# One transformer layer with attention and routed experts: how VectorE inverts the softmax sums and assigns expert slots

## The reference

```
q = x Wq                     16 heads of 64;  latent = x Wkv_down (64 columns)
k, v = latent Wk_up, latent Wv_up
attn = softmax(mask(q k^T / 8));  y = attn v;  x = layernorm(x + y Wout)
probs = softmax(x w_router)  32 experts;  top1 = argmax;  gate = probs[top1]
pos = rank of the token among those of its expert (cumsum of the one-hot rows) - 1
slot = top1 * 320 + pos      where pos < 320, else dropped
out = (silu(buf w_gate[e]) * (buf w_up[e])) w_down[e] for the 320 rows of each expert e
x = layernorm(x + out[slot] * gate, or x alone where dropped)
```

## Time and profile before

| | |
|---|---|
| Time, median of 3 runs | 2606.3 us (2603.69 to 2608.29) |
| The profiled execution's own time | 2605.42 us |
| Its span | 2603.4 us |
| Busy: TensorE, VectorE, GpSimd, ScalarE | 2364.8, 1697.2, 1678.0, 1029.3 us |
| TensorE's mean granted clock | 0.96 of full speed |
| VectorE's copies L1150 in all | 210.6 us in 256 |

### The profile page before, as it was taken

The page is one execution under the profiler, slowest core; times in us unless marked ns, Lnnn a source line. Parts: engine busy times, 40 slices in busy tenths (PEclk is TensorE's granted clock), DMA queues, the critical chain, the costliest instruction groups (busy, mean ns, idle before and its releaser), DMA issues.

```text
span 2603.4 us, 36668 instructions
## 1 busy us (share of the span) xinstructions
PE 2364.8 (91%) x11528; PEld 1519.9 (58%) x11528; DVE 1697.2 (65%) x4490; ACT 1029.3 (40%) x1992; POOL 1678.0 (64%) x1623
## 2 busy tenths in 40 slices
PE   6899998999988998999889998899899988959996
PEld 5555575556655665557555664566555755546774
DVE  4677667676676667776767677666777576434554
ACT  3444424443344434442444344443444244312222
POOL 1677656766677767765777667766687577722444
PEclk8999999999999999999999999999899999969998
DMA  3122100200011001100020001100110001215662
GB/s 84 58 62 70 46 13 13 66 17 17 13 41 42 17 13 25 58 17 13 13 66 18 17 14 43 39 17 13 25 58 17 13 13 49 74 39 163 187 194 67
DMA packets 96816, 118.95 MB, mean 46 GB/s; under 512 B 12288, under 2 KB 75782, under 8 KB 96624
## 3 DMA queue, kind: packets, MB, share of 16 engines
q1 hardware_dynamic: 89712, 99.98, 14.0%
q0 software_dynamic: 6912, 16.64, 1.8%
HBM read 46.91 MB, written 37.90 MB: 33 GB/s over the span
## 4 chain that ended last, share of the span: by engine, by line
PE 54%; POOL 21%; issue 14%; DVE 5%; ACT 1%; POOLq 0%; DMA 0%; DVEq 0%; SPq 0%; ACTq 0%
PE value_ps L721 13%; POOL half_sums L503 12%; PE turned_ps L698 6%; PE misc_ps L743 6%; PE turned_ps L890 5%; PE turned_ps L701 5%; PE misc_ps L620 4%; PE row_ps L673 4%; POOL probs L478 3%; PE misc_ps L733 3%; PE turned_ps L673 2%; POOL slots_x L535 2%; POOL half_sums L498 2%; POOL headsT L510 1%; DVE rinv_rows L1154 1%
## 5 line engine op out<-in xcount | busy, mean ns | idle before, releaser
L963 ACT ACTIVATE probs<-turned_ps 128x512 f32<-128x512 f32 (+2 forms) x1280 | 652.5, 554 | 806.0 <-PE turned_ps L701 787.6
L503 POOL TENSOR_TENSOR half_sums<-half_sums,probs 128x1024 f32<-128x1024 f32 (+3 forms) x512 | 829.6, 1620 | 33.2 <-ACT probs L963 15.9
L721 PE MATMUL value_ps<-probs,lat_keys 128*64 128x512 f32 (+3 forms) x3072 | 610.7, 513 | 70.9 <-POOL probs L478 66.3
L698 PE MATMUL turned_ps<-q_hl,lat_hi 128*128 128x512 f32 (+2 forms) x1280 | 534.5, 418 | 1.5 <-ACT fold_v L1008 1.5
L478 POOL TENSOR_SCALAR_AFFINE_SELECT probs<-probs 128x256 f32<-128x256 f32 x512 | 208.3, 407 | 465.1 <-ACT probs L963 464.3
L701 PE MATMUL turned_ps<-q_max,lat_lo 65*128 65x512 f32 (+2 forms) x1280 | 486.5, 380 | 2.8 <-DMA q_max<-both_rows 2.8
L1116 DVE CUSTOM_DVE_ANT_0 masked_row<-row_ps,future 128x512 bf16<-128x512 f32 (+4 forms) x707 | 346.9, 511 | 150.4 <-PE row_ps L673 144.4
L721 PEld LDWEIGHTS value_ps<-probs,lat_keys 128*64 128x64 f32 x3072 | 185.0, 139 | 357.5 <-issue 203.7
L673 PE MATMUL row_ps<-lat_hi,q_hl 128*128 128x512 f32 (+4 forms) x1026 | 321.0, 353 | 48.7 <-DVE unit_max L1116 37.0
L498 POOL TENSOR_TENSOR half_sums<-probs 128x768 f32<-128x768 f32 (+1 forms) x128 | 269.2, 2103 | 136.2 <-ACT probs L963 113.3
L698 PEld LDWEIGHTS turned_ps<-q_hl,lat_hi 128*128 128x128 f32 x1280 | 248.1, 194 | 166.7 <-issue 100.6
(11 more groups left out here) (192 smaller groups left out, 2664.7 us busy)
## 6 DMA issues: line engine op xcount, KB each, us to landing
q_max<-q_hl SPq DMA_DIRECT2D x256, 128.0 KB
slots_x<-router SPq DMA_DIRECT2D x8, 1290.0 KB, 5.9
ex_x<-slots_x SPq DMA_DIRECT2D x64, 129.0 KB, 2.3
x_in<-in_L_attn_x_bld SPq DMA_DIRECT2D x8, 1024.0 KB, 5.5
layer_out<-x_in SPq DMA_DIRECT2D x8, 1024.0 KB, 4.6
ex_w<-in_L_ffn_w_gate SPq DMA_DIRECT2D x32, 256.0 KB, 3.8
ex_w<-in_L_ffn_w_up SPq DMA_DIRECT2D x32, 256.0 KB, 3.7
ex_w<-in_L_ffn_w_down SPq DMA_DIRECT2D x32, 256.0 KB, 4.5
```

What stands on the lines that cost most here:

```text
L503: nc.gpsimd.tensor_tensor(total, total, now[:, :, q0:BANK], ALU.add).then_inc(added, 1)
L698: nc.tensor.matmul(scores_of(n, h), lat_hi[b % 2][:, keys], q_hl[gp % 2][:, heads, cols], start=True, stop=False)
L721: mm = nc.tensor.matmul(value_ps[h * LD:(h + 1) * LD, q0:BANK], lat_keys[b % 2][:, j, :], probs[:, n % NPROBS, h, q0:BANK], start=(j == 0) ...
L963: nc.scalar.activation(probs[:, n % NPROBS, heads, q0:BANK], scores_of(n, h), ACT.Exp).then_inc(exp_done, 1)
```

## The change

In `invert_rows` the one reciprocal of 128 partitions, the wait behind it and the two copies become four reciprocals of 32 partitions each, straight from `sums_cols`: for each head the group of the half c is read twice and written once onto itself and once onto the head's other group. The transposes wait for all four.

`place` is cut into three functions. `place` (pair 3, t = 7) keeps the product that frees the bank, now first, and two sums over experts. `count_tiles` (pair 3, t = 9, after `low_q`) has the counts, their addition to `earlier` and the inverse of the router's sum. `destinations` (pair 3, t = 11) has the rest. For the last batch all three stand one behind the other.

```diff
                 wait_emptied(dve, ("sums", gp))
-                nc.vector.reciprocal(rinv[:, c, :], sums_cols[:, :].rearrange("p (n q) -> p n q", q=32)[:, :, 0]
-                                     ).then_inc(inverse_done, 1)
-                dve.wait_ge(inverse_done, 3 * n + 1)
+                cols = sums_cols[:, :].rearrange("p (n q) -> p n q", q=32)[:, :, 0]
                 for h in range(2):
-                    src, dst = (64 * h + 32 * k for k in (c, 1 - c))
-                    nc.vector.tensor_copy(rinv[dst:dst + 32, c, :], rinv[src:src + 32, c, :]).then_inc(inverse_done, 1)
-                dve.wait_ge(inverse_done, 3 * n + 3)
+                    src = slice(64 * h + 32 * c, 64 * h + 32 * c + 32)
+                    for k in range(2):
+                        dst = slice(64 * h + 32 * k, 64 * h + 32 * k + 32)
+                        nc.vector.reciprocal(rinv[dst, c, :], cols[src]).then_inc(inverse_done, 1)
+                dve.wait_ge(inverse_done, 4 * (n + 1))
...
                 dve.wait_ge(gate_exp, b + 1)
-                step(nc.vector.tensor_reduce(rt[:, 1, :], work_b[:, :, :], AX.X, ALU.add))
-                settle()
-                step(nc.vector.reciprocal(rt[:, 2, :], rt[:, 1, :]))
                 bank = wait_full(dve, use)
                 nc.vector.tensor_tensor(work_a[:, :, :], onehot[:, :, :],
                                         bank[:, 0:NT * E].rearrange("p (t e) -> p t e", e=E), ALU.mult
                                         ).then_inc(free_of(use), 1)
+                step(nc.vector.tensor_reduce(rt[:, 1, :], work_b[:, :, :], AX.X, ALU.add))
                 wait_emptied(dve, use)
+                step(nc.vector.tensor_reduce(rt[:, 4, :], work_a[:, :, :], AX.X, ALU.add))
+
+            def count_tiles(b):
 
                 step(nc.vector.tensor_reduce(in_tiles[:, :], onehot[:, :, :].rearrange("p t e -> p e t"), AX.X, ALU.add))
                 settle()
                 step(nc.vector.tensor_tensor(earlier[:, :, :], earlier[:, :, :],
                                              in_tiles[:, :].unsqueeze(1).to_broadcast([P, NT, E]), ALU.add))
-                step(nc.vector.tensor_reduce(rt[:, 4, :], work_a[:, :, :], AX.X, ALU.add))
+                step(nc.vector.reciprocal(rt[:, 2, :], rt[:, 1, :]))
+
+            def destinations(b):
+
                 settle()
-
...
+                    if b and (p, t) == (3, 9):
+                        count_tiles(b - 1)
+                    if b and (p, t) == (3, 11):
+                        destinations(b - 1)
...
+                if use[0] == "pos":
+                    count_tiles(LAST)
+                    destinations(LAST)
```

## The result

| | before | after |
|---|---|---|
| Median | 2604.99 us (4 runs, 2603.6 to 2608.29) | 2541.97 us (4 runs, 2539.83 to 2543.32) |
| Ratio | | 0.9756 [0.9739, 0.9772] |
| Profiled span | 2603.4 us | 2539.1 us |
| TensorE busy / not busy in it | 2364.8 / 238.6 | 2347.1 / 192.0 |
| VectorE, GpSimd busy | 1697.2, 1678.0 | 1595.7, 1680.1 |

The forecast was 2542 us. The span fell by 64.3 us: 46.6 of them are idle time of TensorE, and 17.7 are busy time, though the matmuls are the same. Most of the second part goes with its clock. Between the first and the last transpose L1137 the record of the granted clock has TensorE at half the clock (1.2 of 2.4 GHz) for 109.2 us before and for 71.7 after. It was busy in 100.1 and 71.7 of them: 28.4 us fewer, which at half speed is 14 us of work.

A forecast was written before the change was run, and what follows sets the result against it. Attention was taken as bound by TensorE's order of work. Gains 31.8 + 2.4 + 30 - 0.45 = 63.8 us from 2605.4 gave 2541.6, median 2542.5, forecast 2542; own range 2528 to 2558, widened to 2526 to 2566.

The forecast's parts named there:

- my upper end of 0.97: Inversion: four reciprocals in a line, each waiting for the last, 0.97 us; wholly overlapped 0.24, taken 0.72.
- The `low_q` stall: Pair 6: TensorE awaits the q subtraction 1.04 us; a third, 0.35 us, back in each of seven, 2.4 us.
- The 34.4 us taken off for pair 3: Share of TensorE's 66.2 us row-score waits lying in pair 3 of batches 1 to 7, left to the split of `place`.
- 31.8 + 2.4 = 34.2: Gain from quicker inversions outside pair 3: 31.8 us of stalls behind inversions, 2.4 us at pair 6's q subtraction.
- Rival (a): GpSimd's select before value products takes over, 1.00 us stalls return in some 18 pairs: gain 46, 2560 us; chance 0.10.
- Priced by its neighbour: Pair 3 priced from pair 4's 32.3 us: 32.0 us instead of 36.3, gain 4.3 in seven batches, 30 us.
- They should still be in time: Pair 3, t = 11: next pair's first row maxima and GpSimd's sends, queued behind the moved operations, would not be late.
- rival (b): Pieces of `place` cost what the whole cost, sends come late, pair 3 keeps 36.3 us: gain 34, 2572 us; chance 0.07.
- the 4 of my bound: Pair 3, t = 11: if three dependent groups each wait for GpSimd, 0.8 us becomes 4 at most.
- The end: Last batch: a 0.41 us reduction now follows the position matmuls, +0.45 us; the four reciprocals there cost 0.
- (c): Slower: reciprocals writing another partition group each wait for a GpSimd operation of their own: +51 us, 2657; chance 0.03.
- (d): Stalls go but time does not, since TensorE's clock falls when it idles less: 2606 us; chance 0.02.

The follow-up runs named there:

- e5: Changed kernel, but each reciprocal reads the group of partitions it writes, so half of the inverses belong to the wrong queries; 2539.7 us, one run.
- e10: Changed kernel with one reciprocal and two one-element maximum reductions per inversion, and counts and destinations moved to t = 8; 2509.99 us, ratio 0.9633 to the kernel before.
- e8: Changed kernel with counts and destinations at t = 8, behind the second inversion, instead of t = 9 and 11; 2533.31 us.
- e7: Changed kernel with the old single reciprocal and two one-element maximum reductions in place of the old two copies; 2530.96 us.
- e9: Kernel before with only its two copies per inversion replaced by one-element maximum reductions, `place` whole; 2524.38 us, ratio 0.9685.
- e2: Kernel before with only the four reciprocals in `invert_rows`, `place` left whole at t = 7; 2547.3 us, ratio 0.9773.
- e6: Changed kernel with four copies from the transposed sums in place of the four reciprocals; 2617.53 us, ratio 1.006 to the kernel before.

## Why the prediction was right, and where by luck

**The inversions.** Right that the copies wait for GpSimd and reciprocals never do (512 at 230 to 254 ns), with or without a change of groups (e5), and that the 1.00 us stalls go. Wrong in size: I took 0.16 us between starts as for operations that overlap, and the four come 0.27 us apart: 1.10 us from first to transpose, above my upper end of 0.97. That leaves 0.15 us in 19 places, 3.1 us. The `low_q` stall, of which I expected 2.4 us back, went from 5.8 to 7.3. (The 34.4 us taken off for pair 3 should be 34.6, 7 times 4.94; it changes nothing.) And yet pairs 4 to 6, batch 0 and the last two pairs gave 34.3 (pairs 0, 1 and 7 took 0.5 back), against 31.8 + 2.4 = 34.2. So this term came out by luck in part: the stalls themselves gave less than I counted. Beside them stand the 17.7 us of busy time over the whole kernel, most of it at half the clock, for which I had priced nothing here; how much of it fell in these pairs' favour is not shown.

**What is late next.** I had TensorE's waits for the select go up to 75 us; they fell to 59.1. Rival (a), GpSimd takes over, is refuted for this kernel: GpSimd's wait for `rinv_rows` is 0.27 us in the pair shown where it was 1.12, and the idle time ahead of its select stays (2.38 us where it was 2.41). Not all of GpSimd's waits before L510 went, as I had put among the signs: they sum to 58.2 us after and 87.3 before, and many are still 0.7 to 1.6 us. In e10, where the last stalls are gone, the handover does happen (77.6).

**Pair 3.** Priced by its neighbour at 32.0, it came out at 32.85: 25.3 us, not 30. The steps up to t = 9 were right: the addition 1.16 us (its ends were 0.42 and 2.22), the stall behind it 1.53 (1.6 taken), the stalls together about the 2.8 that the neighbour waits. What failed is the price by the neighbour. Two pairs with the same idle time do not last the same: pair 3 at 3.12 us idle and pair 4 at 3.36 are alike, but TensorE's busy time is 29.68 and 27.84; the position matmuls are 0.55 of that and the clock, 0.95 and 0.98, most of the rest. Nor is the clock the whole miss, since the one batch without a fall of it took 32.44 us. Against pair 4 (31.07) and the 0.55, that is 0.8 us, where I had 0.2 for late moves at t = 11. In e8 and e10, where those operations stand at t = 8, pair 3 takes 31.76 and 31.29. "They should still be in time" was wrong of the sends: they wait 0.9 to 1.3 us for the destinations, six times (6.6 us). That was one of my signs of being wrong, and a part of rival (b). The operations of t = 11 took 3.3 to 3.6 us from the first to the last, not the 0.8 that I had put in the sum, near the 4 of my bound: L1248 0.90, then L1252 1.30 to 1.33 in five batches and L1255 1.18 to 1.20 in the other two. The Trainium skill ("SBUF — State Buffer", Who interferes with whom) had them contend; the trace agrees (L1252 at 0.17 us in e8, 1.31 beside GpSimd). I had written that the trace of before shows no tensor_scalar beside GpSimd. It does, in seven of sixteen places of L1193:

```profile
L1193 DVE TENSOR_SCALAR var_eps<-mean_var x16: 170/170/1191, 362.7 to 2307.5; 128x4 f32<-128x4 f32 x16
```

It takes 0.17 us, and 1.19 beside GpSimd, so the cost of t = 11 could have been read before.

By the same section a tensor_reduce does not contend on trn2: e7 and e9 agree, at 156 to 166 ns in 256 places.

**Pair 2.** Its 4.8 us are in no step. They are the stretches at half the clock: 34.1 us of them begin in pair 2 before, 23.9 after, and its idle time is the same (0.26 and 0.25 us). So a term 5 us too large and one 5 us too small stood on the two sides of the sum, and that they cancelled is luck. The end was priced at +0.45 and measured at -0.3, but the changed kernel's second run took 309.5 us for it and not 309.0, so that a difference as small can't be told.

**Rivals.** (b) did not come: e2, where the `place` stays whole, is 2547 and not 2572, so its price rested on pair 3 keeping 36.3, while the inversion alone brings it to 34.14. (c) did not come for reciprocals; copies do wait, but mostly once for a group and not once each (e6). (d) is refuted, and has the wrong sign: with fewer stalls the clock was at half its speed for 71.7 us and not 109.2.

What stays open: why the clock falls in one batch and not in the next at the same place, and how much of the 46.6 us of idle time and of the 17.7 us of busy time belong to which stall. No run holds the one fixed while it changes the other.

## What to carry to other kernels

Where a small VectorE operation shows a median far under its longest time, and the longest is as long as GpSimd's operation, replace the kind of operation before the order of the work: here a copy as a maximum over one element gave 80 us, four reciprocals 58, and the moving of `place` 8 more or 7 less. Put the small operations that can't be replaced where the timeline shows GpSimd idle, and then read the busy time of TensorE beside its waits: the same lateness of another engine shows as idle time at full clock and as busy time at half clock (pair 3 of the changed kernel, 32.44 and 32.46 us). The worth of one part of a change is not fixed: the split gave 20 us with copies, 8 to 10 with reciprocals and a loss with reductions.

## What was not expected of the hardware

- Four independent reciprocals of 32x16 do not overlap: 244 ns each, 0.27 us from start to start (1.06 us in all). Reductions of the same shape take 160 ns.
- A reciprocal that writes another group of partitions than it reads costs the same 244 ns (e5 against the kernel after).
- Tiny operations wait as whole ones do: a tensor_scalar of 128x8 took 0.16 us alone and 1.3 beside GpSimd's operations, a scalar_tensor_tensor 0.17 and 0.9, in e9 1.9.
- In pair 3, TensorE fell to 1.2 GHz around stalls of 1.2 to 3.4 us in a stream that is otherwise busy: in six of seven batches behind a stall of 1.21 us (e9), in five and in one of seven behind a stall of 1.75 us (e8, e10).
- What such a stretch costs depends on what is late behind it: nothing in one batch (changed kernel, pair 3 in 32.46 us with it and 32.44 without), 0.8 us in another kernel (e8, 31.96 and 31.12).
